# A grouped convolution on Trainium2: stores issued from ScalarE's DMA queue, loads and taps from SyncE's alone

## What is computed

```
def _L0_conv_ref(x, weight, bias):
    x_cat = jnp.concatenate([x, x[:, :, :-1, :]], axis=2)
    out = jax.lax.conv_general_dilated(x_cat, weight, window_strides=(1, 1), padding='VALID', dimension_numbers=('NCHW', 'OIHW', 'NCHW'), feature_group_count=x.shape[1])
    return out + bias[None, :, None, None]

def _gn(v, G=32, eps=1e-5):
    B_, C_, H_, W_ = v.shape
    g = v.reshape(B_, G, C_ // G, H_, W_)
    m = jnp.mean(g, axis=(2, 3, 4), keepdims=True)
    s = jnp.var(g, axis=(2, 3, 4), keepdims=True)
    return ((g - m) / jnp.sqrt(s + eps)).reshape(v.shape)

x = x + _L0_conv_ref(_gn(x), L0_conv_weight, L0_conv_bias)
```

## Time and profile before

| | |
|---|---|
| time, median of 3 runs | 844.32 us (842.21 to 863.63) |
| time of the profiled execution | 843.1 us |
| its span, first to last instruction | 841.4 us |
| granted TensorE clock, mean | 0.995 of full speed |
| busy: PE, PE weight loads | 706.6 us (84%), 555.5 us (66%) |
| busy: DVE | 727.6 us (86%) |
| busy: ACT | 661.6 us (79%) |
| busy: POOL | 574.5 us (68%) |
| DMA | 336.57 MB, mean 400 GB/s |

### The profile page before, as it was taken

The page is one execution under the profiler, slowest core; times in us unless marked ns, Lnnn a source line. Parts: engine busy times, 40 slices in busy tenths (PEclk is TensorE's granted clock), DMA queues, the critical chain, the costliest instruction groups (busy, mean ns, idle before and its releaser), DMA issues.

```text
span 841.4 us, 8606 instructions
## 1 busy us (share of the span) xinstructions
PE 706.6 (84%) x1920; PEld 555.5 (66%) x1920; DVE 727.6 (86%) x1602; ACT 661.6 (79%) x1026; POOL 574.5 (68%) x1114
## 2 busy tenths in 40 slices
PE   0699889888887888988888988888988888987895
PEld 0477667666666666766666767666766667766684
DVE  7799988888888888889998899998888998898862
ACT  0799878777787777878878988887887887887893
POOL 3388667767676666766766776776776676775775
PEclk9999999999999999999999999999999999999998
DMA  8999999999999999999999999999999999999977
GB/s 349 411 350 400 411 411 414 416 422 409 412 413 396 402 402 390 398 403 410 414 418 415 417 413 419 425 418 420 418 414 419 422 418 414 410 420 404 391 243 248
DMA packets 37572, 336.57 MB, mean 400 GB/s; under 512 B 4624, under 2 KB 4752, under 8 KB 6800
## 3 DMA queue, kind: packets, MB, share of 16 engines
q1 hardware_dynamic: 37520, 336.02, 98.9%
HBM read 181.86 MB, written 154.14 MB: 399 GB/s over the span
## 4 chain that ended last, share of the span: by engine, by line
DMA 57%; DVE 19%; ACT 11%; issue 6%; POOL 5%; PE 1%; SPq 0%; POOLq 0%
DMA xt<-x 31%; DMA out<-xt 26%; DVE st L280 10%; ACT xn L355 7%; DVE xt L304 5%; ACT kept L364 3%; POOL xt L248 3%; DVE runs L289 2%; PE conv L428 1%; DVE runs L288 1%; POOL newt L240 0%; POOL newt L239 0%; POOL rstd L241 0%; POOL shift L242 0%; POOL newt L238 0%
## 5 line engine op out<-in xcount | busy, mean ns | idle before, releaser
L428 PE MATMUL conv<-xn,runs 128*128 128x448 f32 x1536 | 662.3, 574 | 64.7 <-ACT xn L355 48.7
L428 PEld LDWEIGHTS conv<-xn,runs 128*128 128x128 f32 x1536 | 511.3, 347 | 147.4 <-ACT xn L355 77.0
L280 DVE BATCH_NORM_STATS2 st<-xt 128x6 f32<-128x336 f32 x1024 | 451.9, 495 | 84.8 <-DMA xt<-x 83.3
L248 POOL TENSOR_TENSOR xt<-xt,kept 128x448 f32<-128x448 f32 x384 | 434.7, 1139 | 104.5 <-ACT kept L364 104.5
L355 ACT ACTIVATE xn<-xt,shift,rstd 128x672 f32<-128x672 f32 x512 | 462.7, 942 | 47.2 <-POOL shift L242 47.2
L304 DVE SCALAR_TENSOR_TENSOR xt<-conv,bias_all,xt 128x448 f32<-128x448 f32 x384 | 257.0, 669 | 17.9 <-PE conv L428 17.8
L364 ACT ACTIVATE kept<-conv,bias_all 128x448 f32<-128x448 f32 x384 | 232.8, 620 | 9.6 <-PE conv L428 9.4
L345 ACT ACTIVATE std<-var,eps 128x8 f32<-128x8 f32 x64 | 19.2, 301 | 97.3 <-DVE var L294 97.2
L404 PEld LDWEIGHTS p_mean<-msum,neg_mean 128*128 128x128 f32 x128 | 19.9, 193 | 94.5 <-POOL msum L217 80.2
L404 PE MATMUL p_mean<-msum,neg_mean 128*128 128x8 f32 x128 | 25.2, 269 | 59.2 <-POOL msum L217 59.2
L238 POOL TENSOR_TENSOR newt<-r 128x8 f32<-128x8 f32 x64 | 12.7, 198 | 62.1 <-DVE r L299 61.4
(11 more groups left out here) (31 smaller groups left out, 97.2 us busy)
## 6 DMA issues: line engine op xcount, KB each, us to landing
xt<-x SPq DMA_DIRECT2D x128, 1344.0 KB, 16.0
out<-xt SPq DMA_DIRECT2D x128, 1176.0 KB, 14.3
runs<-taps SPq DMA_DIRECT2D x32, 168.0 KB, 13.5
bias_all<-bias SPq DMA_DIRECT2D x1, 192.0 KB, 13.8
```

What stands on the lines that cost most here:

```text
L248: nc.gpsimd.tensor_tensor(cell, cell, kept_of(u, c), ALU.add).then_inc(pool_added, 1)
L280: ins = nc.vector.bn_stats(st[:, n % RS, h, b, :], xt[0:P, n % XS, h, b * ROW:(b + 1) * ROW])
L428: nc.tensor.matmul(bank(c), lay[:, :, c], channel_of(xn, u % NS, c), start=True, stop=True).then_inc(conv_ready, 1)
```

## The change

The stores leave SyncE. `store` is now a function of ScalarE's program with the same two waits (`dve_taken`, `pool_added`), issued from ScalarE's own DMA queue: store (u,0) between the evictions of channels 9 and 11 of unit u, store (u-1,1) in unit u behind the copy of the negated mean, and the last store behind the loop. SyncE's loop runs over loads: load (n,0) and load (n,1), each waiting for its half-slot's `out_stored`; behind the pair of an odd n come the taps of group (n - 6) // 2 + 2, with a wait until unit n-6 is convolved. The taps of group 31 come in a loop at the end. SyncE's last waits for all stores stay.

```
-            def store(u, h):
-                last = (h + 1) * CH - 1
-                sp.wait_ge(dve_taken, through(DVE_CH, u, last))
-                sp.wait_ge(pool_added, through(ACT_CH, u, last))
-                sp.dma_start(out[u, :, h, :], xt[EDGE:EDGE + DATA, u % XS, h, :]).then_inc(out_stored[u % XS][h], 16)
-
...
-            for u in range(UNITS):
+
+            for n in range(XS, UNITS):
                 for h in range(HALVES):
-                    store(u, h)
-                    g = u // PER_GROUP + 2
-                    if h == 1 and u % PER_GROUP == PER_GROUP - 1 and g < GROUPS:
-                        load_taps(g)
-
-                    if u >= 1:
-                        load(u - 1 + XS, h)
+                    load(n, h)
+
+                g = (n - XS) // PER_GROUP + 2
+                if n % PER_GROUP == PER_GROUP - 1 and g < GROUPS:
+                    sp.wait_ge(conv_ready, (n - XS + 1) * CG)
+                    load_taps(g)
+            for g in range((UNITS - XS) // PER_GROUP + 2, GROUPS):
+                sp.wait_ge(conv_ready, (g - 1) * PER_GROUP * CG)
+                load_taps(g)
...
+            def store(u, h):
+                last = (h + 1) * CH - 1
+                act.wait_ge(dve_taken, through(DVE_CH, u, last))
+                act.wait_ge(pool_added, through(ACT_CH, u, last))
+                act.dma_start(out[u, :, h, :], xt[EDGE:EDGE + DATA, u % XS, h, :]).then_inc(out_stored[u % XS][h], 16)
...
                 evict(u, ACT_CH[0])
                 if m < UNITS:
                     negmean(m)
+                if u >= 1:
+                    store(u - 1, 1)
                 if n < UNITS:
                     normalize(n, 2, 4)
...
-                for c in ACT_CH[4:]:
-                    evict(u, c)
+                evict(u, ACT_CH[4])
+                store(u, 0)
+                evict(u, ACT_CH[5])
+            store(UNITS - 1, 1)
```

## The result

The changed kernel takes 980.79 us (median of 4 runs, 976.34 to 983.47), against 848.54 us of the kernel before (4 runs beside it): a ratio of 1.158, with a 95% interval of 1.147 to 1.169. Executions come in a faster and a slower state; ratios go by the faster ones alone, the medians by all. It is slower, by more than the 944 us that were forecast, and inside the range of 860 to 990. The profiled execution took 976.34 us with a span of 974.6, 133 us more than before.

What follows compares the result with a forecast made beforehand. DMA, 99% occupied, bound the kernel; now late taps would set the pair. First such store 57.6, 29 pairs x 28.9 = 838.1, end 46.2: span 942; plus 1 for ScalarE's stores and 1.7: 945, given as 944 us; range 860 to 990.

Steps and rivals of the forecast that it cites:

- The bound, and the slack of the taps: DMA engines 99% occupied; taps, issued 13.2 us ahead of their layout, land in a median of 13.5, just in time.
- T: Time of a pair of units, S + e; 28.9 us forecast, at least the 25 us of the transfers.
- S: Time from an odd unit's second store to the taps' layout on VectorE; 17.5 us forecast, 13.6 before.
- e: Time from the taps' layout on VectorE to the next odd unit's second store; taken as 11.4 us.
- How the two queues share: While both DMA queues hold work, each gets half of the rate; row-wise sharing, 944 us, chance 0.68.
- whole transfers alternate: Rival: the two DMA queues alternate by whole transfers, not rows; T 26.7 us, total 881 us; chance 0.14.
- served in order of issue: Rival: transfers of both queues go in order of issue, S no longer binds; 829 to 843 us; chance 0.12.
- Landed 17.1 to 18.3: When the taps land, in us after the odd unit's second store is issued; gave S = 17.5.
- the term of 1 us: Stores on ScalarE: 0.3 us of waiting in each of the last four units, 1 us added; range 0 to 60.
- Part 3: Earlier loads buy nothing; VectorE's 83.3 us of waits for loads fall to nearly 0, reappearing as 180 us for taps.
- the signs: VectorE's taps copy waits 28 or 29 times, 5 to 7 us each; stores land in about 8, loads 8 or 9.
- The faster rival: Rival: taps in time, loads and stores mix better; at 430 GB/s a pair takes 24.4 us, total 814; chance 0.06.

Runs made afterwards that it cites:

- e1: Changed kernel with the taps issued ahead of the two loads of that turn; 832.4 us, ratio to the kernel before 0.977.
- e2: Kernel before, one queue, with the taps issued later, behind the first load instead of right behind the store; 930.3 us, ratio to the kernel before 1.091.
- e7: Changed kernel with the taps issued between the two loads; 886.3 us, ratio to the kernel before 1.054.
- e10: Changed kernel, taps still behind both loads, with three buffers for taps instead of two; 838.9 us, ratio to the kernel before 0.986.
- e8: e1 with store (u,0) moved on ScalarE from behind the fifth eviction to behind the fourth; 832.5 us, ratio to the kernel before 0.991.
- e6: Changed kernel with the taps issued by ScalarE, right behind store (v,1) in the stores' queue; 852.9 us, ratio to the kernel before 1.015.
- e9: e1 with three buffers for taps instead of two; 837.0 us, ratio to the kernel before 0.984.
- e11: e1 measured again, against the kernel before in more rounds; 831.8 us, ratio 0.979.
- e4: Changed kernel with the taps of groups 0 and 1 alone loaded, later loads and their waits left out; 816.0 us, ratio to the kernel before 0.957.
- e3: Kernel before with the taps of groups 0 and 1 alone loaded, later loads and their waits left out; median 851.4 us (830.2 to 866.6).

## Why the prediction was right, and where its sizes were off

**The bound, and the slack of the taps: right.** The step that found the loss was to set the taps' 13.5 us of landing against the 13.2 that they had, and to follow where the new program puts them. e1, e2, e7 and e10 show it from four sides. That T is S + e follows from how the two are cut out and shows nothing by itself; what the runs show is that e stays at 9.8 to 11 us while S takes up the delay. The means of 29 pairs, with the taps' issue behind store (v,1) as a median:

| kernel | taps issued, us | S | e | T |
|---|---|---|---|---|
| before | 0.4 | 14.5 | 11.0 | 25.4 |
| e7 | 3.8 | 16.0 | 10.7 | 26.7 |
| e2 | 5.5 | 18.7 | 9.8 | 28.5 |
| changed | 6.3 | 20.1 | 9.9 | 29.9 |

**How the two queues share: right.** The prediction assumed that while both hold work each gets half. A stretch of the changed kernel with both at work (us, busy times, clock, DMA share, GB/s), and what the two queues moved in it:

```profile
429.00:433.00 4.00, 3.24 (x10) 2.27 (x9) 2.73 (x6) 3.27 (x6) 3.84 (x8) 1.00 1.00 417
```

```profile
q1 hardware_dynamic: 87, 0.90, 53.1%
q10 hardware_dynamic: 78, 0.76, 46.7%
```

Joined end to start, the packets of this stretch fall into 16 chains, as many as there are DMA engines, and in 12 of them rows of loads and rows of stores alternate one by one; in the other four they start at the same instants as a neighbour's and can't be told apart. This is what the Trainium skill's page "DMA: Bandwidth & Descriptors" says in "Queues, rings and completion order", round robin at packet granularity, and here the trace agrees, with one row of 10,752 bytes to a turn. The two rivals by which whole transfers alternate, or are served in order of issue, fall by the same rows.

**The size of S: 17.5 forecast, 20.3 measured.** The step that was off is the landing of the taps: 14.0 us here (13.6 in the median) where 9.5 to 10.7 was worked out, in the line "Landed 17.1 to 18.3". Up to the taps' issue the working was near, in part by luck. Store (v,0) landed 1.1 us after store (v,1) was issued, as forecast, though it had gone out 5.6 us ahead and not 4.3. The taps went out at 6.3 us instead of 7.6. What the working lacks is that a transfer ends with its slowest engine: it had sixteen equal ones. The sixteen increments of the taps' semaphore came between 434.9 and 439.9 us. The middle ones came at 435.7, 16.1 us after the store, so for an engine in the middle the working's 17.1 to 18.3 was even 1 us too long; the last one came at 20.3. In the median over the pairs the middle is 16.6 and the last 19.8. Load (v+6,1), ahead of the taps, landed at 17.9 instead of 16.3 in the same way. Why some engines are late isn't known.

A second assumption failed too, but cost nothing on this way. Here are 4 us with stores almost alone:

```profile
420.00:424.00 4.00, 4.00 (x14) 3.24 (x14) 4.00 (x10) 3.98 (x6) 2.62 (x6) 1.00 0.94 282
```

Load (v+6,0) is issued at 420.73, and still the trace has 107 packets in the stores' queue and one in the loads': the load's rows begin some 3 us after its issue, not 1.5. The engines do 282 GB/s at a share of 0.94, so that a store's row takes some 0.56 us, where 417 GB/s was assumed. The 318 GB/s in the earlier trace rows had pointed there. But store (v,1) had no load beside it and landed at 5.9, before the 7.2 of the working.

**The size of e: 11.4 forecast, 9.8 measured.** The 11.4 came from two pairs of before, 11.6 and 10.8; the mean of 29 is 11.0. The layout's copies took 2.1 us before at 405.99 and take 0.7 now, 57.1 us in 64 copies before and 25.5 now; that POOL is idle when they come, and no longer in their way, is argued and not tested. This took back 1.6 of the 2.8 us that S was short, which is luck.

**The sum.** From 942 to 974.6 us of span are 32.6: 29 pairs of 29.9 instead of 28.9 make 30, the first store 1.0 us later and an end that is 2.0 us longer make the rest. Small slips in the prediction's own sums don't matter to this: the loads that wait for a store are 116, not 122; S of 16 makes 901 us, not 895, and T of 25 makes 831 or 832, not 829; and from 945 to 944 no step leads.

**The DMA share: 0.87 forecast, 0.95 measured** (100 to 700 us, above), at 354 GB/s. Rows take longer than before the change: 451 ns in the loads' queue and 469 in the stores', against 419. That a stall lines the stores up, and that stores alone are slow (0.56 us a row, above), fits this and wasn't tested further. In any case the share of time can't be read as a share of capacity.

**ScalarE: the term of 1 us was right, its parts not.** In the timeline above the store with h = 0 is issued at 414.08, before the normalization at 414.14 and the first of the two evictions from 414.98, both of which stand ahead of it in the program; the next one goes out at 425.35 in the same way. So it isn't 3 us late: it comes 4.3 us behind the layout, where 3.6 stood before, right behind the wait for the root's variance, which ends at 413.94. Of the work ahead of it in the program it waits for the semaphores, not for the execution. The store with h = 1 waits for its semaphore, and the engine runs dry: 0.72 us of idle time before the normalization at 420.01, in the waits above as 22.5 and 20.6 us for the takes and adds in 61 places. That is 0.7 us a unit, near the 0.32 of issue and 0.3 of waiting that were forecast for this store, and it falls into ScalarE's slack, since e1 has it too (44.3 us in 61 places) and is faster than the kernel before.

**Part 3: right.** VectorE's wait for x fell to 3.2 us, and came back as a wait for taps, 231.6 us where 180 was forecast. Stores land in 7.5 us and loads in 9.1, as the signs had it (8, and 8 or 9); the 29 waits are 8.0 us each in the mean, not 5 to 7.

**What was missed:** with the taps in time the kernel with two queues can be faster than the one before, by 2.3% (e1) on one chip; e8, much the same kernel, gains 0.9% on the other, and e6 loses 1.5% there. The faster rival had this with a chance of 0.06 and on that condition. And the chain of waits reads badly here: it hands the taps to a convolution.

```profile
422.01 3.90 PE conv L435 x10
425.91 13.99 DMA runs<-taps
```

The taps' instruction waits on the counter of convolutions, which had passed its mark a unit earlier; it kept counting, and its last step before 425.91 is named. What SyncE really waited for was the landing that released the load at 425.53.

## What to carry to other kernels

Before a transfer is moved behind a wait in an in-order queue, set what it takes to land under load against the time to its first reader; where both are 13 us, most of any delay is lost once per use: taps issued 3.4, 5.1 and 5.9 us later made the pair 1.3, 3.1 and 4.5 us longer (e7, e2, the changed kernel). A small transfer (here 2% of the bytes) is best put ahead of the large ones that wait, or given one more buffer, which mends it in any order. With that in place, loads on one queue and stores on another were 0.9 to 2.3% faster than all in one (e8, e1, e9 to e11), but not where the taps went with the stores (e6). And a transfer that somebody waits for is priced by its slowest engine, not by the mean of the sixteen.

## What the runs showed of the hardware

- With both queues holding work, rows of 10,752 bytes from the two alternated one by one in at least 12 of 16 chains of packets (429 to 433 us of the changed kernel, 87 and 78 packets).
- The sixteen engines finished one transfer 5.0 us apart (taps, 434.9 to 439.9 us), 4.5 us in the median; the landing is that of the last.
- A DMA's issue in ScalarE's program went out ahead of work that stands before it: the store at 414.08 ahead of a normalization and an eviction that began at 414.14 and 414.98. In units 3 to 59 each such store went out at least 0.6 us before the eviction ahead of it began. Waiting for a semaphore that wasn't met drained the engine (0.72 us).
- At a DMA share of 1.01, loads and stores in two queues gave 413 to 425 GB/s (e6 413, e10 417, e1 422, e4 425), in one queue 413 and 414 (the kernel before, e3); stores with almost nothing beside them gave 282 at 0.94.
- Around TensorE's waits of 4 to 5 us stood 3.4 to 10 us at the lower clock; filling the wait with matmuls brought the clock from 0.913 to 0.998 of full speed, and no time.
